# Self attention: a batch's end inside the next batch, maxima at steps 1 to 5, the split of queries and keys on GpSimd, shift rows from two queues, maxima on 48 rows

## What is computed

```python
def _L0_attn_ref(x, norm_w, Wq, bq, Wk, bk, Wv, bv, Wo, bo):     # 16 heads of 8
    xn = x * rsqrt(mean(x * x, -1) + 1e-6) * norm_w
    q, k, v = (heads(xn @ W.T + b) for W, b in ((Wq, bq), (Wk, bk), (Wv, bv)))
    scores = einsum('bhqd,bhkd->bhqk', q, k) / sqrt(8)
    scores = where(causal, -inf, scores)
    out = einsum('bhqk,bhkd->bhqd', softmax(scores), v)
    return xn + merge(out) @ Wo.T + bo

x = x + _L0_attn_ref(_layernorm(x), ...)
x = x + _L0_xattn_ref(_layernorm(x), ctx, ...)
x = x + _L0_ffn_ref(_layernorm(x), ...)
```

## Time and profile before

| | us |
|---|---|
| runs: median (lowest to highest of 3) | 1709.92 (1709.72 to 1713.21) |
| profiled run, device time | 1708.21 |
| its span | 1706.4 |
| PE busy in the span | 1517.9 (89%) |
| DVE, ACT, POOL busy | 1119.9, 917.8, 563.4 |
| first to sixth unit 0 inside the loop of self attention | 99.89 to 253.37 |
| start of cross attention's first unit | 311.03 |

### The profile page before, as it was taken

One profiled execution on the slowest core, in us unless ns is written; L12 is line 12 of the kernel. 1 busy time (PEld: TensorE's weight loads), 2 busy tenths in 40 slices (PEclk: granted clock), 3 DMA queues, 4 the chain that ended last, 5 costly groups with the idle time before them and its releaser, 6 DMA issues. The chain is left out here.

```text
span 1706.4 us, 29542 instructions
## 1 busy us (share of the span) xinstructions
PE 1517.9 (89%) x10917; PEld 828.5 (49%) x10941; DVE 1119.9 (66%) x2531; ACT 917.8 (54%) x1996; POOL 563.4 (33%) x695
## 2 busy tenths in 40 slices
PE   1667768899999999999999998899999999899998
PEld 1334434344444444444444443566666676544443
DVE  4855543878788787878787883566666655465554
ACT  1233325376777677777777776355555555333443
POOL 4210013030303012030303000688888788133331
PEclk9988879799999999999999999899999999899999
DMA  4232225223122323242232210000000000000001
GB/s 97 63 70 43 57 56 126 54 87 53 71 51 43 102 50 102 49 102 50 88 52 73 49 27 4 10 1 1 1 1 1 2 1 1 4 21 22 20 20 34
DMA packets 76978, 75.04 MB, mean 44 GB/s; under 512 B 12196, under 2 KB 66340, under 8 KB 75940
## 3 DMA queue, kind: packets, MB, share of 16 engines
q1 hardware_dynamic: 76836, 73.16, 19.0%
HBM read 42.47 MB, written 30.16 MB: 43 GB/s over the span
## 5 line engine op out<-in xcount | busy, mean ns | idle before, releaser
L1296 DVE TENSOR_REDUCE b_chunk_max<-psum 128x1 f32<-128x400 f32 x1004 | 530.6, 569 | 140.8 <-PE psum L1495 133.7
L1424 ACT ACTIVATE b_prob<-psum 128x512 f32<-128x512 f32 (+1 forms) x832 | 450.5, 594 | 182.1 <-PE psum L1532 176.2
L1495 PE MATMUL psum<-k_stack,q_stack 128*128 128x400 bf16 x1004 | 276.7, 340 | 10.1 <-DMA k_stack<-b_k_scratch 4.9
L1504 PE MATMUL psum<-b_prob,b_v_aug 128*32 128x256 f32 (+1 forms) x3328 | 265.8, 391 | 1.7 <-ACT b_prob L1424 0.4
L1532 PE MATMUL psum<-q_stack,k_stack 128*128 128x256 bf16 (+1 forms) x1664 | 254.1, 275 | 3.7 <-ACT b_prob L1424 3.3
L1532 PEld LDWEIGHTS psum<-q_stack,k_stack 128*128 128x128 bf16 (+1 forms) x1664 | 145.8, 99 | 123.0 <-ACT b_prob L1424 75.7
L1691 POOL TENSOR_SCALAR c_prob<-c_prob,c_rec 128x128 f32<-128x128 f32 (+1 forms) x256 | 192.3, 770 | 9.7 <-POOL c_kT L1700 8.6
L2106 DVE TENSOR_TENSOR e_hg<-e_gl,e_gate 128x512 f32<-128x512 f32 x124 | 122.9, 1013 | 89.0 <-PE psum L2154 84.4
L1774 DVE SCALAR_TENSOR_TENSOR c_turned<-psum,c_bias,c_tab 128x256 f32<-128x256 f32 x256 | 106.1, 476 | 112.7 <-PE psum L1907 112.7
L1809 ACT ACTIVATE c_prob<-psum,c_mneg 128x128 f32<-128x128 f32 (+1 forms) x256 | 104.1, 418 | 137.6 <-DVE c_mneg L1751 137.6
L2046 ACT ACTIVATE e_gl<-psum,b1T 128x512 f32<-128x512 f32 x124 | 85.2, 687 | 127.6 <-PE psum L2149 125.9
(11 more groups left out here) (236 smaller groups left out, 1950.7 us busy)
## 6 DMA issues: line engine op xcount, KB each, us to landing
k_stack<-b_k_scratch SPq DMA_DIRECT2D x32, 600.4 KB, 10.2
b_k_scratch<-b_kparts SPq DMA_DIRECT2D x7, 1200.8 KB, 4.4
b_k_scratch<-b_kparts SPq DMA_DIRECT2D x7, 800.5 KB, 6.1
b_ctxT<-in_ctx SPq DMA_DIRECT2D x8, 600.4 KB, 11.8
e_w<-in_L_ffn_re_w SPq DMA_DIRECT2D x62, 64.0 KB, 1.9
a_scratch<-a_parts SPq DMA_DIRECT2D x16, 192.0 KB, 2.1
q_stack<-b_q_scratch SPq DMA_DIRECT2D x32, 96.0 KB, 2.2
b_k_scratch<-b_kparts SPq DMA_DIRECT2D x7, 400.2 KB, 6.7
```

The source lines that it names most:

```text
L1296: nc.vector.tensor_reduce(out=chunk_max[:, half, q, column4(hh), c:c + 1], in_=max_bank(v)[:, 0:w], axis=AX.X, op=ALU.max).then_inc(max_do ...
L1424: nc.scalar.activation(prob[0:k, buf, par * 2 * T:(par + 1) * 2 * T], st_bank(v, par)[0:k, :], ACT.Exp, scale=HD ** -0.5).then_inc(exp_don ...
L1495: nc.tensor.matmul(max_bank(T_.now("unit"))[:, 0:hi - lo], queries_of(qst, h, slice(q * P, q * P + P)), keys_of(kst, h, slice(lo, hi)), st ...
L1504: last = nc.tensor.matmul(pv[32 * hh:32 * hh + 32, :], v_aug[0:k, kt, g * GH + hh, :], prob[0:k, buf, c:c + T], start=(kt == 0), stop=(kt ...
```

## The change

The steps of a batch are no longer a closed block. A batch's last values, last "pv", "attnT" and "out" now stand in steps 0 to 2 of the next batch; a ninth block of three steps ends batch 7, and early units follow it. The residual gets a third buffer, and the semaphore of stack loads one per parity. The maxima of b+1 are made at steps 1 to 5 (1, 3, 3, 3 and 2 units), and "m" follows in step 5.

ACT writes queries and keys twice, in f32 and as the first bf16 part; POOL makes the other two parts with three operations. The first shift row leaves from ACT's queue (two DMAs), the second from SP (two DMAs).

The maxima matmuls take only the 48 rows of their head (`tile_position`), and the mask comes last and covers the 128 diagonal columns of each head. The scores' mask covers 128 columns a head too. Masks are merged from four tiles to two. The rotary weights and biases come from the host in both orders; they are loaded with the other rotary weights at the start of cross attention, POOL's reordering is gone, and two POOL memsets move.

```diff
-        ITEMS_AT = {0: "v", 2: "x", 3: "pv", 4: "qk", 5: "pv", 7: "pv"}
-        UNITS_AT = [range(n * UNITS // STEPS, (n + 1) * UNITS // STEPS) for n in range(STEPS)]
+        UNITS_AT = [range(lo, hi) for lo, hi in ((0, 0), (0, 1), (1, 4), (4, 7), (7, 10), (10, 12), (12, 12), (12, 12))]
+        def items_of(b, n):
+            late, more, further = b >= 1, b + 1 < B, b + 2 < B
+            items = {0: [("pv", b - 1, late)], 1: [("attnT", b - 1, late)],
+                     2: [("out", b - 1, late), ("x", b + 2, further)], 3: [("pv", b, b < B)], 4: [("qk", b + 2, further)],
+                     5: [("pv", b, b < B), ("m", b + 1, more)], 6: [], 7: [("pv", b, b < B)]}[n]
+            return [(kind, of) for kind, of, there in items if there] + early.ITEMS.get((b, n), [])
...
-    UNITS = {(7, 6): range(0, 4), (7, 7): range(4, 8), (7, "last"): range(8, 12), (7, "pv"): range(12, 16),
-             (7, "attnT"): range(16, 20)}
+    UNITS = {(7, 6): range(0, 4), (7, 7): range(4, 8), (8, 0): range(8, 12), (8, 1): range(12, 16), (8, 2): range(16, 20)}
...
+            def split(b):
+                pool.wait_ge(qk_ready, b + 1)
+                own(nc.gpsimd.tensor_tensor(rest[:], qk[:], parts[:, 0, :], ALU.subtract))
+                own(nc.gpsimd.tensor_tensor(parts[:, 1, :], rest[:], early.zeros[:], ALU.add))
+                nc.gpsimd.tensor_tensor(parts[:, 2, :], rest[:], parts[:, 1, :], ALU.subtract).then_inc(parts_ready, 1)
...
+                    for m in range(2):
+                        part = slice(m * T, m * T + T)
+                        nc.scalar.activation(qk[:, part], prep[:, part], ACT.Identity, bias=bqk[:, m:m + 1])
+                        last = nc.scalar.activation(parts[:, 0, part], prep[:, part], ACT.Identity, bias=bqk[:, m:m + 1])
...
-                    nc.tensor.matmul(bank, identb[:], t[mask][:].rearrange("p h k -> p (h k)"), start=True, stop=False)
                     for n, h in enumerate(heads):
-                        last = nc.tensor.matmul(bank[:, n * keys:(n + 1) * keys], queries_of(qsts[j], h, slice(q * P, q * P + P)),
-                                                keys_of(ksts[j], h, slice(0, keys)), start=False, stop=(n == len(heads) - 1))
+                        part = rows_of(h, NP * HD)
+                        nc.tensor.matmul(bank[:, n * keys:(n + 1) * keys], qsts[b % 2][part, h, q * P:q * P + P],
+                                         ksts[b % 2][part, h // 2, 0:keys], start=(n == 0), stop=False, tile_position=(part.start, 0))
+                    nc.tensor.matmul(bank.rearrange("p (h k) -> p h k", k=keys)[:, :, keys - P:keys], identb[:],
+                                     t["mask_qk"][:, 0:len(heads), :], start=False, stop=True).then_inc(max_full, 1)
```

More of the change, by code:

```diff
@@ L256, in load @@
         nc, a = self.nc, self.a
[L257 to L269, removed]
+        for quarter in range(4):
+            rows = slice(32 * quarter, 32 * quarter + 32)
+            sp.dma_start(self.theta[rows, :], a["L0_ffn_theta"].rearrange("(p a) -> p a", a=1)).then_inc(self.loaded, 16)
+    N_LOADS = 4
     def positions(self, pool):
         self.nc.gpsimd.iota(self.posi[:], pattern=[[1, T]], base=0, channel_multiplier=0).then_inc(self.pos_set, 1)
[L274 to L280, removed]
     def angles(self, dve):
@@ L461, in self_attention, with program @@
         ones_set, stack_cleared, passed = sem("a_ones_set"), sem("a_stack_cleared"), sem("a_passed")
-        PER = {name: 2 * n for name, n in dict(
-            item=3 + 1 + G + 2, norm=2, next=1, batch=1, stack=1, m=1, qk=1, unit=UNITS, scores=STEPS, values=STEPS, group=G,
-            dve_own=NORM_LINKS + RMS_LINKS + 3 + G + 2, pool_own=QT).items()}
+        qk_ready = sem("a_qk_ready")
+        PER = ("item", "norm", "next", "unit", "dve_own", "pool_own", "qk", "m")
         block = ctx.enter_context(nc.Block())
-        def shown(kind, more, further):
-            return {"v": more, "x": further, "qk": further, "m": more}.get(kind, True)
-        def program(eng, tally, begin, attend):
+        def program(begin, attend):
             begin()
[L476 to L480, removed]
+            for b in range(B + 1):
+                attend(b)
         @block.sync
@@ L513, in attend @@
                     bounce_parts(sp, early.q_scr, early.qparts[:], 0, early.q_bounced)
[L514 to L520, removed]
+                if b + 1 < B:
+                    store_m(b + 1)
+                if b + 2 < B:
+                    stack(b + 2)
                 if b == B - 2:
@@ L583, in begin @@
             def begin():
+                nc.gpsimd.memset(early.zeros[:], 0.0).then_inc(early.ones_set, 1)
+                pool.wait_ge(early.ones_set, 1)
                 for j in range(2):
                     powers()
-                    residual(j, j)
+                    residual(j)
+                    split(j)
                     if j == 0:
@@ L698, in maxima, with attend @@
                     nc.vector.tensor_reduce(out=dst, in_=src, axis=AX.X, op=ALU.max, negate=True).then_inc(max_done, 1)
[L700 to L703 removed]
+            def attend(b):
+                for n in steps_of(b):
+                    if n == 0 and b + 1 < B:
+                        item("v", b + 1, 0)
+                    if b + 2 < B:
                         norm(b + 2, n)
@@ L983 @@
+            program(begin, attend)
 class Tally:
```

362 lines of the change are left out of this document (176 added, 186 removed).

## The result

The changed kernel takes 1730.01 us (median of four runs, 1723.60 to 1742.25) against 1709.82 before: a ratio of 1.0133, 95% interval 1.0108 to 1.0158. It is slower by some 20 us; 1714 was forecast, with 1723 as the upper end. The profiled execution is the longest of the four (span 1740.5), so its stretches are to be read for what they hold, and not added up to the median.

The account below looks back on a forecast made before the run. A chain of waits, first maxima unit to first maxima unit, bounds each batch. Start -2.4, five rounds +2.6, batches 6 and 7 +1.5 and +2.0, rotary weights +0.3: +4.0 on 1708.2, 1712.2; median 1.7 above, 1714 us, range 1701 to 1723.

Parts of the forecast that it names:

- The clock is in it as it is today: Around a batch's first maxima unit: granted clock stays 0.50 until 4 us behind that unit, as in the kernel before.
- The leg from the first unit to the projection: From a batch's first maxima unit to the query and key projection: grows from 10.83 to 13.7 us.
- the price of its changes: Array form changes between 128 and 48 rows in maxima units: 0.09 us each, twenty a batch, +2.1 us.
- the prediction's second rival: Changes to 48 rows cost nothing, first unit to projection takes 11.6 us: about 1703 us, chance 0.24.
- Bounce to stack: From SP's bf16 part stores to its stack load: falls from 8.93 to 4.41 us, a gain of 4.5.
- Projection to bounce: From query and key projection to SP's stores, with POOL's split: 6.57 us against 4.40, a loss of 2.2.
- Stack to first unit: From SP's stack load to the next batch's first maxima unit: stays 6.36 us.
- The batch's end: Moving a batch's last work into the next batch's steps 0 to 2: brings nothing while the stack load ends last.
- Start: Before the loop: the next batch's first maxima unit comes at about 97.5 instead of 99.89, -2.4 us.
- Batches 6 and 7: Last self-attention batches, up to cross attention: +1.5 us for batch 6 and +2.0 for batch 7.
- The array pays more for its changes: Form changes cost 0.15 us or more, or reductions hold units: round 32.5 us, about 1721, chance 0.20.
- A clock that stays up: Full clock around a batch's first maxima unit: about 2 us a round gained; no chance of its own given.

Follow-up runs that it names:

- control with 64-column tiles: The kernel before, with maxima heads on all 128 rows as two side-by-side tiles of 64 columns: 1718.93 us, 1.0063.
- both parts undone: The changed kernel with maxima heads on 128 rows again and VectorE making the split of queries and keys again: 1686.95 us, 0.9876.

## Why the prediction was wrong

The step that failed is the sentence on the clock: "The clock is in it as it is today". The leg from the first unit to the projection was given 13.7 us, with ends of 11.6 and 15.2. Where the clock rose about 4 us behind the first unit, as it was taken to do, the leg takes 13.03 and 13.07; where it rose later (mean clock 0.50 to 0.61), 16.6 to 19.2. So the sum of its work and the price of its changes (0.09 forecast, 0.10 measured, 10 us in the control with 64-column tiles) held nearly. The stretch at half speed was taken over from the kernel before as if it were a property of the batch, and it moves with what PE does: with 48 rows it went on through 9.53 us of work without a gap. So the 48 rows cost 22.5 us where about 10 were given, for their changes of form. With 128 rows and all else as changed the time is 1707.5; the prediction's second rival, without that price, said 1703.

The other steps, one by one:

- *Bounce to stack* fell to 4.50 as forecast (4.41), but in every other batch only to 6.16, through slow issue on SP that the rows at the start didn't show. The early maxima that it stands for are worth 16 us in the kernel with both parts undone (1703.09 to 1686.95), with what they add to the next leg; five times 4.5 would have been 22.
- *Projection to bounce:* 6.46 measured (7.35 in one of five rounds), 6.57 forecast; the three operations are 1.15, 1.26 and 1.16, where 3.54 were given to their sum of 3.57. Its price was too low all the same. Taking it back gives 20.5 us with 128 rows (1707.48 to 1686.95) and 27 with 48, where the leg of 2.15 in five rounds and the start is 13. In the profiles with 128 rows the leg from the first unit to the projection falls by 0.7 a round beside it, and batches 6 and 7 by 3 us; whether the clock does that is not shown.
- *Stack to first unit* stayed at 5.9 to 7.1 (6.36).
- *The batch's end* brings nothing, as forecast, but not because it is hidden: once the other legs are short its move makes each of five rounds 1.6 us shorter, and batches 6 and 7 longer by 8.6 (see below), where 2.0 was forecast.
- *Start:* the first unit of batch 1's round was forecast at 97.5 and stands at 102.12 in the profile; with 128 rows it comes at 91.9.
- *Batches 6 and 7:* +3.5 was forecast for both, +18.4 is in the profile, more than in the five rounds together. With 128 rows the two take 67.3 us instead of 76.1, so about half of the loss goes with the rows. The other half is near what the end's move costs there, 8.6 in the kernel with both parts undone. From batch 6's first unit to the next batch's scores the profile has 313.12 - 271.51 = 41.6 us against 30.1, where +1.5 was forecast; PE works there at a mean clock of 0.57:

```profile
271.51:311.00 39.49, 33.52 (x169) 14.58 (x170) 11.29 (x23) 12.58 (x23) 11.58 (x12) 0.57 0.22 70
```

- *The rivals.* "The array pays more for its changes" had the right sign and came nearer, 1721, but for the wrong cause: a change costs 0.10, not 0.15. A clock that stays up was weighed as a rival; one that stays down was not.

From run to run the parts are -4 us (what else was changed, with the end's move in it: the run with late maxima, 128 rows and VectorE's split, at 0.9977 of the kernel before), -16 for the early maxima, +20.5 for giving up VectorE's split, and +22.5 for the 48 rows. These are steps of one path from the kernel before to the changed one, so that they add up (+23; the measured ratio of 1.0133 is +22.7) confirms nothing. The price of a part depends on the others: the 48 rows cost 15.7 us with VectorE's split (1686.95 to 1702.68), 22.5 with GpSimd's and 21.5 in the kernel before.

## What to carry to other kernels

A price for work on PE holds at one clock, and here a change of the matmuls' form moved the clock itself. So count the busy time of such a stretch at both levels, and take the lower one as an end of the range. Where a chain bounds the loop, a step that is moved off a half-idle engine pays its full latency, and here it paid more (20.5 to 27 us for 13 of latency). And of a change made of several parts, undo them one at a time before giving it up: without two of its parts this one is 1.2% faster than the kernel before, and 2.5% faster than the changed one.

## What the runs showed of the hardware

- With heads on 48 of 128 rows PE was busy for 9.53 us without a gap and was still granted 0.50; in one of five legs it was granted 1.00 after 4.4 us. With all rows in the same kernel it was granted 1.00 after 3.9 to 4.3 us, and with all rows in two tiles of 64 columns after 3.1 to 5.8 us.
- A change between a 128-row and a 48-row form took 0.10 us at full clock.
- On SP one of the bounce's six stores took 1.4 to 1.9 us to issue in place of about 0.5, in every second batch of the changed kernel, with or without other stores on ACT's queue.
